# Self-attention of a decoder layer: the mask moved from TensorE to VectorE, and the output's projection split between the transposes

## The reference

```python
x = layernorm(x + self_attention(x, Wq, Wk, Wv, Wo))     # 16 heads of 32, rotary q and k, causal mask
x = layernorm(x + cross_attention(x, ctx, ctx, gamma))   # 8 heads, over features
x = layernorm(x + ffn(x, w1, b1, ln_g, ln_b, w2, b2))    # BitLinear 512-2048-512, silu, gelu, layer norm
```

```python
q, k, v = x @ Wq.T, x @ Wk.T, x @ Wv.T                   # split into 16 heads, q and k rotated
scores = q @ k.T / sqrt(32)
scores = where(causal, scores, -inf)
out = softmax(scores) @ v
return out @ Wo.T
```

## Time and profile before

| | |
|---|---|
| median of 3 runs | 1848.72 us |
| lowest, highest | 1835.46, 1850.77 us |
| the profiled execution | 1833.27 us |
| its span in the trace | 1831.5 us |
| busy over the span | PE 88%, DVE 84%, ACT 75%, POOL 52% |
| instructions of PE, DVE, ACT, POOL | 11936, 2086, 2853, 1408 |
| the chain that ended last | PE 58%, issue 12%, DVE 10%, ACT 7%, DMA 6%, POOL 5% |

### The profile page before, as it was taken

The page is one execution under the profiler, slowest core; times in us unless marked ns, Lnnn a source line. Parts: engine busy times, 40 slices in busy tenths (PEclk is TensorE's granted clock), DMA queues, the critical chain, the costliest instruction groups (busy, mean ns, idle before and its releaser), DMA issues.

```text
span 1831.5 us, 35203 instructions
## 1 busy us (share of the span) xinstructions
PE 1609.7 (88%) x11936; PEld 873.5 (48%) x12000; DVE 1546.8 (84%) x2086; ACT 1377.0 (75%) x2853; POOL 961.4 (52%) x1408
## 2 busy tenths in 40 slices
PE   6999999999998889999999999999777777767774
PEld 4777777777775333333333333333233333333331
DVE  5788888888887989999989899999489999899985
ACT  4666645555453578888888888888699999899994
POOL 6667667676674533355544555323445555545542
PEclk9999999999999799999999999999878888888886
DMA  3465443434337454444464654444333333333311
GB/s 136 147 183 175 127 120 112 136 105 130 115 117 189 109 105 112 108 118 120 108 175 131 168 120 118 108 118 104 118 98 104 104 105 104 104 104 104 104 47 35
DMA packets 119269, 217.10 MB, mean 119 GB/s; under 512 B 32241, under 2 KB 34705, under 8 KB 116785
## 3 DMA queue, kind: packets, MB, share of 16 engines
q1 hardware_dynamic: 110770, 213.64, 41.5%
q0 software_dynamic: 8320, 1.21, 0.4%
HBM read 137.67 MB, written 76.02 MB: 117 GB/s over the span
## 4 chain that ended last, share of the span: by engine, by line
PE 58%; issue 12%; DVE 10%; ACT 7%; DMA 6%; POOL 5%; SPq 1%; POOLq 0%; DVEq 0%; ACTq 0%
PE sums L1059 13%; PE bank L1076 12%; PE bank L549 11%; PE wide L1029 6%; PE sums L549 5%; DMA out<-c_result 3%; PE wide L599 3%; DVE stage L1710 2%; ACT stage L1595 2%; PE wide L591 2%; ACT b_prob L945 2%; DVE a_prob L469 2%; PE sums L611 2%; DMA b_xs<-b_max_part 2%; PE wide L586 1%
## 5 line engine op out<-in xcount | busy, mean ns | idle before, releaser
L969 DVE TENSOR_REDUCE b_smax<-wide 128x2 f32<-128x1024 f32 x512 | 620.5, 1225 | 60.4 <-PE wide L1029 48.6
L945 ACT ACTIVATE b_prob<-bank 128x512 f32<-128x512 f32 x1024 | 556.3, 599 | 111.6 <-PE bank L1076 101.1
L1076 PE MATMUL bank<-b_xs,b_cs 50*128 50x512 f32 x1024 | 329.5, 478 | 23.6 <-ACT b_prob L945 13.2
L1059 PE MATMUL sums<-b_prob,b_vT 128*32 128x256 f32 (+1 forms) x3584 | 318.8, 428 | 5.2 <-ACT b_prob L945 0.5
L1029 PE MATMUL wide<-b_cs,b_xs 48*128 48x512 f32 x1024 | 282.8, 436 | 9.1 <-DVE b_smax L969 7.6
L1888 PE MATMUL sums<-c_w,c_hqT 128*128 128x512 bf16 x481 | 170.2, 530 | 114.1 <-issue 106.8
L1076 PEld LDWEIGHTS bank<-b_xs,b_cs 50*128 50x128 f32 x1024 | 133.4, 187 | 234.4 <-ACT b_prob L945 172.6
L885 POOL TENSOR_SCALAR b_max_part<-b_neg_max 16x128 fp32r<-16x128 f32 x64 | 18.6, 291 | 322.6 <-ACT b_neg_max L936 322.5
L370 ACT ACTIVATE a_prob<-wide,a_neg_max 128x128 f32<-128x128 f32 x512 | 181.8, 417 | 3.9 <-DVE a_neg_max L461 3.9
L1888 PEld LDWEIGHTS sums<-c_w,c_hqT 128*128 128x128 bf16 x512 | 63.4, 128 | 210.8 <-issue 185.9
L895 POOL DMA_DIRECT2D b_xs<-b_max_part x256 | 134.2, 530 | 42.1 <-POOL b_max_part L888 37.3
(11 more groups left out here) (147 smaller groups left out, 3247.7 us busy)
## 6 DMA issues: line engine op xcount, KB each, us to landing
scratch_c_part<-a_c_part SPq DMA_DIRECT2D x64, 256.0 KB
scratch_x_part<-a_x_part SPq DMA_DIRECT2D x64, 256.0 KB
b_xs<-scratch_x_part SPq DMA_DIRECT2D x128, 128.0 KB, 3.1
b_cs<-scratch_c_part SPq DMA_DIRECT2D x128, 128.0 KB, 3.1
scratch_heads<-b_heads SPq DMA_DIRECT2D x64, 256.0 KB, 2.6
a_xT<-in_xT SPq DMA_DIRECT2D x32, 256.0 KB, 6.4
a_c_in<-in_ctx SPq DMA_DIRECT2D x32, 256.0 KB, 2.6
a_x<-in_x SPq DMA_DIRECT2D x32, 256.0 KB, 4.1
```

What stands on the lines that cost most here:

```text
L945: act.activation(prob[k % 8][:, :], e_ps[bank_of(k)][:, :], ACT.Exp, scale=0.25).then_inc(exp_done, 1)
L969: dve.tensor_reduce(smax[g][:, :, j, qc], m_ps[u % 2][:, :, :], AX.X, ALU.max, negate=True).then_inc(max_done, 1)
L1059: last = pe.matmul(av_ps[2 * XD * h:2 * XD * (h + 1), cols], vT[p][:, lc, XG * g + h, :], prob[(XG * n + 2 * j + e) % 8][:, cols], start=( ...
L1076: pe.matmul(e_ps[bank_of(2 * u + e)][:, :], cs[p][g][half(e), j, lc * P:(lc + 1) * P], xs[p][g][half(e), j, :], start=True, stop=True).the ...
```

## The change

The mask goes from PE to DVE. The four mask matmuls of a batch are gone, and each score product is a matmul of its own (start and stop both true). ACT scales q by -1/sqrt(32), so that the scores in PSUM are negated. A tile `barred` holds the negated mask in float32 (ACT makes it once, from one load of the mask in place of four). `maxima` becomes four instructions per group, tensor_tensor_reduce over 128 columns: score plus barred, written to `prob` in SBUF, and the minimum of it, which is the negated maximum, to `neg_max`. `exponentials` works in place on `prob` with the scale -1. The wait for the last transposes of `prob` moves with it from ACT to DVE.

All four copies of the transposed probabilities are ACT's now; DVE's `prob_transposed` is gone, and so is its semaphore. On DVE `out_low` stands ahead of normalise 2. On PE the projection of v stands behind the transposes of probabilities 0, of k and of probabilities 1; the output's projection of t-2 is cut into its three products of four matmuls, `out_third`, which stand ahead of the transposes of probabilities 2, ahead of those of probabilities 3, and ahead of the scores.

```diff
@@ sync
-        for h in range(HPC):
-            sp.dma_start(mask4[:, h, :], t_in["mask"]).then_inc(const_ld, 16)
+        sp.dma_start(mask[:, :], t_in["mask"]).then_inc(const_ld, 16)
@@ scalar
+        act.wait_ge(const_ld, 16 * CONSTS)
+        act.activation(barred[:, :], mask[:, :], ACT.Copy, scale=-1.0).then_inc(barred_done, 1)
...
-                           scale=float(1.0 / np.sqrt(np.float32(DH)))).then_inc(q_raw_done, 1)
+                           scale=float(-1.0 / np.sqrt(np.float32(DH)))).then_inc(q_raw_done, 1)
...
             act.wait_ge(max_done, 4 * b + j + 1)
-            if later(b):
-                act.wait_ge(prob_tr, 4 * b - 3 + j)
             for c in range(KC):
-                last = act.activation(prob[:, j, c, :], s_ps[j][:, c * P:(c + 1) * P], ACT.Exp,
+                last = act.activation(prob[:, j, c, :], prob[:, j, c, :], ACT.Exp, scale=-1.0,
                                       bias=neg_max[:, j, c:c + 1], accum_out=den[:, j, c:c + 1])
...
                 prob_transposed(t - 1, 0)
                 prob_transposed(t - 1, 1)
+            if on(1):
+                prob_transposed(t - 1, 2)
             if on(0):
                 q_transposed(t)
+            if on(1):
+                prob_transposed(t - 1, 3)
@@ vector
+        dve.wait_ge(barred_done, 1)
...
             dve.wait_ge(score_done[j], b + 1)
             if later(b):
-                dve.wait_ge(exp_done, 4 * b - 3 + j)
-            dve.tensor_reduce(neg_max[:, j, :], s_ps[j][:, :].rearrange("p (c n) -> p c n", c=KC), AX.X, ALU.max,
-                              negate=True).then_inc(max_done, 1)
+                dve.wait_ge(prob_tr, 4 * b - 3 + j)
+            for c in range(KC):
+
+                last = dve.tensor_tensor_reduce(prob[:, j, c, :], s_ps[j][:, c * P:(c + 1) * P], barred[:, :], 1.0,
+                                                -MASKED, ALU.add, ALU.min, neg_max[:, j, c:c + 1])
+            last.then_inc(max_done, 1)
...
                 rope_k(t)
+            if on(2):
+                out_low(t - 2)
             if on(1):
                 normalise(t - 1, 2)
                 normalise(t - 1, 3)
-            if on(2):
-                out_low(t - 2)
-            if on(1):
-                prob_transposed(t - 1, 2)
             if on(3):
                 norm_x1(t - 3)
-            if on(1):
-                prob_transposed(t - 1, 3)
@@ tensor
             if later(b):
-                pe.wait_ge(pT_act, 2 * b)
-                pe.wait_ge(pT_dve, 2 * b)
-            for j in range(HPC):
-                pe.matmul(s_ps[j][:, :], ident_b[:, :], mask4[:, :, :].rearrange("p j n -> p (j n)"),
-                          start=True, stop=False)
+                pe.wait_ge(pT_act, 4 * b)
...
                     mm = pe.matmul(s_ps[j][:, c * P:(c + 1) * P], qT[r, c, :], kT[r, c, :],
-                                   start=False, stop=(c == KC - 1))
+                                   start=True, stop=True)
...
+        def out_third(b, n):
+            if n == 0:
+                pe.wait_ge(oT_hi_done, b + 1)
+                if not later(b):
+                    pe.wait_ge(w_lo_done, 4)
+                pe.wait_ge(oT_lo_done, b + 1)
+            a, w = ((oT_hi, wo_hi), (oT_hi, wo_lo), (oT_lo, wo_hi))[n]
+            for c in range(KC):
+                last = pe.matmul(o_ps[:, :], a[:, c, :], w[:, c, :], start=(n == 0 and c == 0),
+                                 stop=(n == 2 and c == KC - 1))
+            if n == 2:
+                last.then_inc(out_done, 1)
...
         def step(t, on):
             if on(0):
                 project(t, 0)
                 project(t, 1)
-                project(t, 2)
             if on(1):
                 transpose_prob(t - 1, 0)
             if on(0):
                 transpose_k(t)
             if on(1):
                 transpose_prob(t - 1, 1)
+            if on(0):
+                project(t, 2)
+            if on(2):
+                out_third(t - 2, 0)
+            if on(1):
                 transpose_prob(t - 1, 2)
             if on(0):
                 transpose_q(t)
+            if on(2):
+                out_third(t - 2, 1)
             if on(1):
                 transpose_prob(t - 1, 3)
             if on(2):
-                out_projection(t - 2)
+                out_third(t - 2, 2)
             if on(0):
                 scores(t)
```

More of the change, by code:

```diff
@@ L94, in self_attention @@
     ident_b = sb("ident_b", [P, P], BF16)
-    mask4 = sb("mask4", [P, HPC, P], BF16)
+    mask = sb("mask", [P, P], BF16)
+    barred = sb("barred", [P, P])
     cos = sb("cos", [P, DH])
@@ L133, in self_attention @@
     const_ld = sem("const_ld")
+    barred_done = sem("barred_done")
     w_hi_done = sem("w_hi_done")
@@ L160, in self_attention @@
     pT_act = sem("pT_act")
-    pT_dve = sem("pT_dve")
     rden_done = sem("rden_done")
@@ L177, in self_attention @@
     dve_passed = sem("dve_passed")
-    CONSTS = 4 + HPC
+    CONSTS = 5
     def sync(sp, begin):
@@ L494, in norm_x1 @@
                               ALU.mult).then_inc(x1_done, 1)
[L496 to L501, removed]
         def step(t, on):
@@ L604, in attend @@
             pe.wait_ge(v_done, b + 1)
-            pe.wait_ge(pT_act, 2 * b + 2)
-            pe.wait_ge(pT_dve, 2 * b + 2)
+            pe.wait_ge(pT_act, 4 * b + 4)
             if later(b):
@@ L613, in attend @@
             last.then_inc(av_done, 1)
-        def out_projection(b):
[L616 to L620, removed]
+        def out_third(b, n):
[10 more added lines that the diff above has]
+                last.then_inc(out_done, 1)
+        def out_projection(b):
+            for n in range(3):
+                out_third(b, n)
         def step(t, on):
```

## The result

The changed kernel takes 1904.12 us in the median of 4 runs (1890.78 to 1910.33), the kernel before, run beside it, 1846.72 us. The ratio is 1.0322, 95% interval [1.0276, 1.0369]: 3.2% slower. The prediction was 1932 us, with a range from 1865 to 1995.

The account below looks back on a forecast made before the run. The prediction took PE to bound the self-attention part, with DVE 3.3 us behind. To the profiled 1833.3 us it added 70 for the wait on k's rotation, 28 for the clock and 1 for the drain: 1932, range 1865 to 1995.

Parts of the forecast that it names:

- The new wait: Self-attention step on PE: k's transpose, now ahead of the value projection, waits for DVE's rotation; step at least 18.35 us.
- R: End of k's rotation on DVE after the step's start: least 7.95 us, forecast 9.5; the step is R + 10.4.
- When DVE comes to the rotation: DVE's maxima, normalisations and rotation end at 9.5 us; step 19.9, 2.25 above 17.65, 70 us over 31 steps.
- the lower bound: Price of each of DVE's 16 new maxima instructions, estimated from below: 0.22 us; the forecast took 0.30.
- What would show it: Signs in the timeline, among them PE idle 2 to 3.5 us before k's transpose and maxima starting after the step does.
- The clock: PE's idle stretch lowers its clock, costing about 1.5 us a time in some self-attention steps; 28 us in all.
- Three steps in five: Share of self-attention steps taken to lose about 1.5 us to the lower clock: 0.9 x 31 = 28 us.
- Rival 1: Self-attention: Vector form cheap (0.22) and clock stays at 2.4 GHz; step 18.6, 1863 us; chance 0.22.
- The rest at about nothing: ACT's copies, exponentials, out-low, POOL, stores and the start cost about nothing; DVE's drain at the end about 1 us.
- Rival 3: Self-attention: the wait for k is covered and the change gains what PE loses in work; with no stall 1792; chance 0.06.
- the 41 us: Saving over 31 steps from removing PE's mask matmuls, were nothing else to happen: 31 x (17.65 - 16.34).
- The sum: Whole kernel: profiled execution plus the later rotation, the lower clock and the drain, 1833.3 + 70 + 28 + 1 = 1932 us.

Follow-up runs that it names:

- e1: The changed kernel with the value projection put back ahead of the transposes, nothing else undone; 1826.21 us, ratio 0.9934 to the kernel before.
- e4: The kernel before with only the value projection moved behind the transposes of probabilities 0, k and probabilities 1; 1874.67 us, ratio 1.0204.
- e7: The changed kernel with only the stores of x_part issued ahead of the load of ctx; 1892.48 us, ratio 1.0309 to the kernel before.
- e3: The changed kernel with the transposes of probabilities 0 done five times over, filling PE's gap; 1864.89 us, ratio 1.0136 to the kernel before.
- e5: e2 with the output's projection in one block ahead of the scores instead of thirds; 1803.72 us, ratio 0.9819 to the kernel before.
- e2: The changed kernel with the value projection ahead again and x_part's stores issued before the load of ctx; 1786.22 us, ratio 0.9740.

## Why the prediction was right, point by point

**The new wait: right.** "What decides is where the value projection now stands" holds. e1 takes it away and turns the loss into a gain; e4 brings it into the kernel before, with nothing else of the change, and the loss is there; e7 shows that no other chain has part in it. The least step that the rows allowed, 18.35 us with R = 7.95, is even the measured one at full clock, but by luck, as two errors cancel: R was 8.33 (8.38 less 0.05), and PE's work from k's transpose on 9.97 us, not 10.33.

**When DVE comes to the rotation: the mis-sized term.** "I take 0.22 + 0.08 = 0.30" was wrong, the lower bound was right: 0.21 from start to start. The Trainium skill (VectorE: DVE Perf Modes, Two Vector instructions with no wait between them) says that an operation which also writes out its accumulator is two instructions. The trace agrees: the read-out of the minimum is there, 0.08 us. But it lies over the next instruction and adds nothing; ACT's 0.09 was no model for it. By the Trainium skill (VectorE: DVE Perf Modes, The TRN2 errata) 120 + columns cycles at 0.96 GHz are 0.26 us, an estimate. The measured spacing of 0.21 is below it and the duration of 0.287 above.

The other two terms ahead of the rotation were high too. The two normalisations took 1.7 us and not 2.2, since POOL now waits for q's copy and is out of their way. The maxima start 0.11 us before the step and not 0.06 after it, against what "What would show it" had named. Together DVE was ready for the rotation 2.0 us earlier than forecast (5.02 after the step's start, not 7.06) and stood waiting for k for 0.8 of them. So any price of the new operation up to 0.21 + 0.80 / 16 = 0.26 us would have given the same step, an estimate from these rows. R = 9.5 became 8.33. The other 0.4 us is PE's work: 17.32 was PE's busy time, and short waits of a few tenths of a microsecond count as busy in it. In the step of the earlier trace rows the last group of transposes passes on to the output's projection only after 0.69 us (425.35 to 426.04), 0.14 after DVE's `out_low` ends (425.90). In e4, where nothing holds it, this passage takes 0.35. The step's 19.9 at full clock became 18.35, and this is 48 us of the sum: 36 of R and 12 of PE's work.

**The clock: right in kind, low in size.** "Three steps in five" were 20 of 29, and the price 1.6 us where I took 1.5: 1.10 us a step against 0.9. e3 shows the cause. Rival 1, which had the low price of the Vector form and the clock at 2.4 GHz, was right in the first half only; with its 18.6 and the measured 1.10 the step is 19.7, nearest of all to 19.47.

**The rest at about nothing: wrong at the start.** "Which covers 2 to 3 us of delay" was a failure to apply what I had read two paragraphs earlier, that DVE and POOL keep each other out. The delay moved DVE's long operations onto POOL's split, and PE started 3.4 us late. The rest of that paragraph held: POOL's and ACT's waits in the changed kernel are waits for PE.

**Rival 3, and the 41 us.** The step without the wait was to be 16.34 us and 31 steps to save 41. Neither number came: with v ahead the step is 17.36, since POOL's chain with the store of x_part, which also ran at 17.6 in the kernel before, takes over. I had given POOL its busy time and left out the store that it waits for, although a wait of it stands in the waits of the kernel before; in the changed kernel this had no effect, because the step was longer than that chain. With the chain out of the way PE needs 15.96, less than 16.34, because waits for DVE that the 17.32 had counted as PE's work are covered by the thirds (e5) and by the earlier `out_low`.

**The sum.** Of the 99 us that I had added, R and PE's work take back 48, the clock adds 31 x 0.2 = 6 and the start 3: 60. By the steps it is the same, 31 x (19.47 - 17.62) = 57 and 3. The medians differ by 57. The profiled executions differ by 72, of which 13 lie behind the last projection of q (1275.5 us from there to the end in the kernel before, 1288.5 in the changed one). e7 has 1273.3 there with the same self-attention but for the order of its stores, so these 13 are not the change's. The sum was thus 42 us too high, and the time only 28, by luck: the profiled execution from which I had started lay 13 us below the median of the kernel before.

## What to carry to other kernels

A block of matmuls that stands between an operation's producer and its consumer is cover; before moving it, write down when its last input and its first output are due, for moving it turned a gain of 1 to 3% into a loss of 3%. When a bound engine is relieved, look for the chain that had just as long a period, DMAs and the queue that issues them included: the same change with the value projection left in place and one block of stores moved up is 2.6% faster, with the tile made late 3.1%. And an idle stretch of TensorE costs more than its own length if its clock falls; here useless work in the gap made the changed kernel 1.8% faster.

## What the runs showed of the hardware that I had not expected

The same idle stretch of PE, 2.15 to 2.17 us by the timeline in almost every step, was followed by half clock (1.2 GHz) in 20 of 29 steps and by full clock in 9; stretches of 1.73 us in each step (e4) or of 0.4 to 0.75 (e3) were never followed by it once the steps were regular. The length alone does not decide: in e1 PE stood idle for 2.14 us once (from 487.1 to 489.2 us, ahead of q's transpose) and for 1.66 in half of its steps, and the clock stayed at 1.00 from 44 to 547 us. What picks the 20 steps is open. Here it gives two step times, about 18.35 and 19.95.

Operations of DVE with two SBUF inputs, one behind the other without a pause, let POOL in only between them: a copy of POOL rose from 0.61 to 2.12 us and a subtraction from 1.26 to 3.18, while DVE's three took 2.29, 2.70 and 3.35. The new operation, with one input in PSUM, left POOL alone: the subtraction for x1 of the step shown (418.82 to 420.10), in which the maxima begin at 419.40, took 1.28 us.

A group of transposes followed by matmuls of 512 columns passes on sooner than one followed by transposes: 0.36 us (the changed kernel's 428.38 to 428.74) against 0.44. But the group of 512 columns behind it takes 0.1 us more than one behind its like (e2: 1.02 against 0.91), so interleaving the two kinds gains PE next to nothing.

The exponentials became slower from SBUF: 0.39 us from one to the next where they had 0.34 from PSUM. ACT had room for it.
